# Third and last attention: scores from 12-bit halves in float32r, their rows spread by DMAs

## The chip, the cores and the metric

One core of one Trainium2 chip runs the kernel. The metric is the device time of one execution in microseconds. The core has TensorE (PE for its matmuls, PEld for its weight loads), VectorE (DVE), ScalarE (ACT), GpSimd (POOL) and SyncE (SP), each with a queue of its own that runs in order, and 16 DMA engines that all queues share. A DMA is issued by an instruction in one of these queues; here SP, ACT and POOL issue DMAs.

## The reference

The input x has 32 sequences of 128 tokens with 128 features. Four blocks follow each other, each an attention and a feed-forward layer with a gated residual. Only the third and the last attention matter here:

```python
# L2: one key head and one value head shared by 16 query heads of 8 features
qh = (q @ w_q).reshape(B, L, 16, 8).transpose(0, 2, 1, 3)
k, v = split(c @ w_kv)                       # 8 features each
attn = softmax(einsum('bhid,bjd->bhij', qh, k) / sqrt(8))

# L3: 16 heads of keys and values, a padding mask and a causal mask
scores = einsum('bhqd,bhkd->bhqk', q, k) / sqrt(8)
scores = where(mask + future != 0, -1e9, scores)
attn = softmax(scores)

x = x + tanh(g) * (attention(layernorm(x), context) @ wo)
```

In both layers the queries come from the normed x, keys and values from the context. Everything is fp32.

## The kernel before

**Stages.** Eight stages run one after the other and overlap at their ends: L0 (attention), F0, L1, F1 (feed-forward with quantised weights), L2 (attention), F2 (experts), L3 (attention), F3. All 32 sequences ("tiles" of 128 tokens) stay in SBUF. The three attentions L0, L2 and L3 share one program, `attention(layer)`, which each engine runs as `iteration(t)`; the tile of the softmax is t, the tile of the first scores t + 2, that of the output projection t - 2. Four tiles make a quad, and `quad(t, lead)` is the number of the quad that begins `lead` tiles ahead, in one iteration of four.

**Scores of one tile.** Each pair of head groups needs its scores twice: once as queries by keys, to find each row's maximum (banks 0 and 1, semaphore `t_s1`, read by DVE's `maxima`, L1744), and once as keys by queries, for the exponentials (banks 2 and 3, `t_s2`, read by ACT's `exponentials`, L960). `pair_of_scores(u, g, v, f)` on PE does one half tile of both: the second kind for tile u and the first kind for tile v = u + 2. The heads of a group of four are told apart by zeros: `k_one` and `q_one` hold four copies of the keys and queries of a quad in which all but one head is multiplied by 0, so that one matmul of 32 partitions by 512 columns gives the scores of four heads (L1284 and L1287). Four such matmuls, one for each group of 32 partitions, follow each other directly. fp32 matmuls appear in the profile as two records. Then L1298 adds minus the maximum, in bf16 parts. In L3, L1274 and L1279 first write the masks into the banks, 16 bf16 matmuls of 32 partitions by 128 columns.

**What waits for what.** Banks 0 to 3 have one buffer: a pair's second kind waits for the exponentials of the pair before it (`t_ex`), its first kind for the maxima of the pair before it (`t_mx`). Between the pairs PE does the weighted values (`weighted_values`, L1316), the output projection and transposes, and once a quad the projections of the next quads: transposes of the normed x (L1382), queries (L1433), keys (L1389), values (L1438).

**ACT's work.** Besides the exponentials, ACT copies what PE projects from bank 5 into `q_all`, `k_all` and `vals`, and makes the four copies of the keys (L970) and of the queries (L976; in L2 only copies 2 and 3, DVE makes 0 and 1 at L1752). `q_all` and `k_all` have two buffers, one for each of two quads.

**Heads.** The first iterations of L2 (t from -10 to -3) are interleaved with the end of F1, by the tables `TENSOR_BETWEEN` and `SCALAR_BETWEEN`, those of L3 with the last expert slots of F2, by `LAST_HEAD`. DVE takes no part in these heads. SP issues no DMA in L2 and none in L3; in F2 it loads experts and rows, and in F3 it stores the output.

## Time and profile before

| | |
|---|---|
| median of three executions | 1081.1 us (1077.25 to 1084.16) |
| span of the profiled execution | 1082.4 us |
| L2, from its first exponentials to its last | about 482 to 668 us |
| L3, the same | about 813 to 1000 us |
| share of PE, DVE, ACT, POOL in the span | 84%, 69%, 63%, 43% |

The span is the time from the first to the last instruction of one profiled execution. It is 1.3 us above the median and inside the range of the three, so sums made against it carry over. A row of a timeline gives the start, the duration, the engine, the line, the operation and what it writes and reads; in brackets stands how long its engine was idle before it and who ended that.

### The profile page before, as it was taken

The numbers are of one execution on the slowest core, as the hardware profiler recorded it, in microseconds if no ns is written. First come the engines' busy times: TensorE is split into PE (matmuls) and PEld (weight loads), VectorE is DVE, ScalarE is ACT, GpSimd is POOL, SyncE is SP. The second block draws the span as 40 slices with busy tenths as digits, with TensorE's granted clock in tenths as the row PEclk, the third lists the DMA queues.
The fourth block names the chain that finished last, engine by engine and source line by source line (L and its number), as shares of the span: only waits on it lengthen the run. The fifth ranks groups of instructions, "written<-read, shape, count | busy, mean of one in ns | idle before, by whom it ended". The sixth has DMA issues, their size and how long they took to land.

```text
span 1082.4 us, 29166 instructions
## 1 busy us (share of the span) xinstructions
PE 913.5 (84%) x9573; PEld 567.0 (52%) x9573; DVE 743.3 (69%) x2005; ACT 684.9 (63%) x1499; POOL 468.1 (43%) x999
## 2 busy tenths in 40 slices
PE   2898888995667856689999989878999899999898
PEld 2744444442345523334555544678864445454698
DVE  2667767765996979967888886337527776666344
ACT  3556666654875656667777764545676677775466
POOL 5422357671124523410144434668651258885200
PEclk9999989996667957799999999999999999999999
DMA  6977677636799997000000000866820001110011
GB/s 175 166 87 100 51 96 86 81 49 135 178 135 165 162 164 94 1 1 2 2 6 12 16 12 12 232 173 188 259 66 22 2 3 41 41 42 2 9 35 36
DMA packets 300444, 84.95 MB, mean 78 GB/s; under 512 B 211930, under 2 KB 287098, under 8 KB 300315
## 3 DMA queue, kind: packets, MB, share of 16 engines
q1 hardware_dynamic: 293962, 67.11, 38.3%
q0 software_dynamic: 5488, 15.88, 4.5%
q8 instruction: 78, 1.28, 0.5%
q14 instruction: 52, 0.42, 0.1%
q10 hardware_dynamic: 864, 0.27, 0.1%
HBM read 50.70 MB, written 35.51 MB: 80 GB/s over the span
## 4 chain that ended last, share of the span: by engine, by line
PE 61%; DVE 22%; issue 8%; POOL 3%; ACT 3%; DMA 2%; SPq 1%; DVEq 0%; ACTq 0%; POOLq 0%
PE bank L1284 16%; DVE nmax L1744 8%; PE bank L1316 7%; PE bank L1406 3%; PE bank L1298 3%; PE bank L1650 3%; PE bank L1642 3%; PE bank L1608 3%; PE bank L1596 3%; DVE small L1926 2%; PE bank L1287 2%; PE bank L1415 2%; PE bank L1274 2%; DVE stats L1679 1%; DVE q_one L1958 1%
## 5 line engine op out<-in xcount | busy, mean ns | idle before, releaser
L1744 DVE TENSOR_REDUCE nmax<-bank 128x8 f32<-128x1024 f32 x192 | 234.8, 1223 | 124.7 <-PE bank L1287 123.2
L960 ACT ACTIVATE probs_space<-bank 128x1024 f32<-128x1024 f32 x192 | 196.5, 1023 | 148.6 <-PE bank L1298 147.6
L1284 PE MATMUL bank<-q_one,k_all 32*128 32x512 f32 x768 | 218.1, 637 | 29.9 <-DVE nmax L1744 26.5
L1287 PE MATMUL bank<-k_one,q_all 32*128 32x512 f32 x768 | 217.4, 640 | 2.2 <-DVE nmax L1744 0.9
L1316 PEld LDWEIGHTS bank<-probs_space,vals 128*32 128x32 f32 x3072 | 73.0, 110 | 123.6 <-issue 122.8
L1316 PE MATMUL bank<-probs_space,vals 128*32 128x128 f32 x3072 | 125.6, 282 | 0.2 <-ACT probs_space L960 0.2
L1284 PEld LDWEIGHTS bank<-q_one,k_all 32*128 32x128 f32 x768 | 62.0, 185 | 59.2 <-issue 57.3
L647 POOL TENSOR_TENSOR var_b<-stats 128x8 f32<-128x8 f32 (+3 forms) x33 | 7.4, 223 | 175.2 <-DVE stats L1679 173.9
L722 POOL CAST nmax_parts<-nmax 128x16 bf16<-128x16 f32 x64 | 12.6, 196 | 160.9 <-DVE nmax L1744 145.5
L970 ACT ACTIVATE k_one<-k_all,one_head 128x512 f32<-128x512 f32 x96 | 68.9, 722 | 20.8 <-DVE k_all L1768 19.3
L1298 PE MATMUL bank<-nmax_one,ones_bf 12*128 12x512 bf16 x384 | 78.6, 381 | 0.0
L1778 DVE TENSOR_TENSOR nmax_one<-bank,max_row 128x512 bf16<-128x512 bf16 x96 | 65.5, 682 | 2.7 <-PE bank L1363 2.7
L1679 DVE BATCH_NORM_STATS2 stats<-x 128x6 f32<-128x128 f32 x230 | 61.3, 287 | 4.2 <-DMA x<-in_x_dram 1.2
L1287 PEld LDWEIGHTS bank<-k_one,q_all 32*128 32x128 f32 x768 | 59.0, 185 | 5.3 <-issue 4.2
L880 POOL DMA_INDIRECT token_rows<-early,slot_row_int x46 | 48.5, 1054 | 29.5 <-DVE early L2114 19.0
L706 POOL TENSOR_TENSOR late<-bf_up,late 128x512 f32<-128x512 f32 x36 | 56.7, 1593 | 0.1
L654 POOL TENSOR_TENSOR var_a<-var_b,minus_half 128x8 f32<-128x8 f32 (+3 forms) x33 | 54.4, 1650 | 2.6
L1608 PE MATMUL bank<-moe_w,probs_space 128*128 x368 | 51.1, 283 | 4.1 <-DVE early L2114 3.7
L976 ACT ACTIVATE q_one<-q_all,one_head 128x512 f32<-128x512 f32 x80 | 54.5, 727 | 0.0
L1608 PEld LDWEIGHTS bank<-moe_w,probs_space 128*128 128x128 f32 x368 | 46.2, 197 | 5.1 <-issue 5.0
L1180 ACT ACTIVATE q_one<-bank,up_bias 128x128 f32<-128x128 f32 x128 | 36.5, 369 | 19.2 <-PE bank L1642 19.2
L865 POOL DMA_INDIRECT expert_rows<-late,dest_int x32 | 32.1, 1004 | 31.6 <-DVE dest_int L1850 24.5
(290 smaller groups left out, 2229.4 us busy)
## 6 DMA issues: line engine op xcount, KB each, us to landing
expert_rows<-zeros SPq DMA_DIRECT2D x8, 2322.0 KB, 38.4
context<-expert_w SPq DMA_DIRECT2D x31, 322.0 KB
k_one<-expert_w SPq DMA_DIRECT2D x15, 322.0 KB
late<-_L_ffn_down_weights_dram POOLq DMA_DIRECT2D x9, 512.0 KB, 5.4
late<-in_L_ffn_up_weights_dram POOLq DMA_DIRECT2D x9, 512.0 KB, 4.0
q_one<-expert_rows SPq DMA_DIRECT2D x46, 64.5 KB
q_scratch<-late SPq DMA_DIRECT2D x8, 256.0 KB
v_scratch<-moe_w SPq DMA_DIRECT2D x8, 256.0 KB
```

The source lines that it names most:

```text
L706: pool.tensor_tensor(tmp(i), half(src, i % 2), weight, ALU.mult).then_inc(S("bf_step"), 1)
L960: act.activation(probs[:, 2 * g:2 * g + 2, :, :].rearrange("k g i q -> k (g i q)"), bank_pair[1][:, :, :].rearrange("k g f -> k (g f)"), A ...
L970: act.activation(k_one[:, c % 2, i, :], k_all[:, c % 2, :], ACT.Copy, scale=one_head[:, i:i + 1]).then_inc(S("t_k1"), 1)
L976: act.activation(q_one[:, c % 2, i, :], q_all[:, c % 2, :], ACT.Copy, scale=one_head[:, i:i + 1]).then_inc(S("t_q23" if i >= 2 else "t_q01 ...
L1284: pe.matmul(bank[2 + s], group(k_all, u, 2 * g + s), group(q_one, u, 2 * g + s), start=not masked, stop=False)
L1287: m = pe.matmul(bank[s], group(q_all, v, 2 * f + s), group(k_one, v, 2 * f + s), start=not masked, stop=True)
L1298: m = pe.matmul(bank[2 + s], ones_bf[first:last, :], nmax_one[first:last, u % 2, :, :], start=False, stop=True)
L1316: m = pe.matmul(bank[4][32 * j:32 * j + 32, g * P:(g + 1) * P], v[:, first:first + VW], probs[:, 2 * g + j // 2, j % 2 * 2 + s, :], start= ...
L1608: m = pe.matmul(bank[(4, 6)[(t - 1) % 2]][:, 0:P], slot_hid[:, (t - 1) % 2, c * P:(c + 1) * P], w2[:, bass.ds(expert[t - 1] * HID + c * P, ...
L1679: dve.bn_stats(stats[:, u, :], x[:, u * P:(u + 1) * P]).then_inc(S("stats"), 1)
L1744: dve.tensor_reduce(nmax[:, u % 2, 0, :].rearrange("q (g i) -> q g i", i=HG)[:, 2 * g:2 * g + 2, :], bank_pair[0][:, :, :].rearrange("q g ...
L1778: dve.tensor_tensor(nmax_one[:, (t + 1) % 2, :, :], over_blocks(bank[6][:, 3 * P:4 * P].bitcast(BF16)[:, 0:P], HG), max_row[:, :].unsqueez ...
```

## The change

In L2 and L3 (`own` in the code) a number is cut in two: `upper` is the fp32 value with its low 12 bits cleared, the other half is the rest. The product of a query and a key is the sum of four products of halves, and these four fill the partitions that were zeros before: in the operands `q_rows` and `k_rows` partition 32 * group + 4 * feature + n holds half `Q_HALVES[n]` of the query or `K_HALVES[n]` of the key. The matmuls read them as float32r. `SCORE_SCALE` moves into the exponentials' `scale`.

- `k_one` and `q_one` copies (L970, L976, L1752) are gone in L2 and L3. DVE splits each quad's keys and queries instead (`halves`: one `bitwise_and`, one `subtract`, each 128 x 512), and holds each once: `q_all` and `k_all` now have one buffer, with the two halves in it.
- DMAs of 32 partitions by 512 fp32 numbers (64 KB), from SBUF to SBUF, spread the halves. For each quad ACT issues 16 for the queries, 8 at the end of iteration `quad(t, 4)` and 8 at the end of `quad(t, 3)`, each time behind the exponentials of that iteration. SP issues those of the keys, 4 per quad in L2 and 16 in L3.
- PE waits for all of a quad's DMAs (`operands_in`) before the first scores of that quad, in `quad(t, 2)`. ACT waits for the same before it overwrites the staging for the next quad (`staging_free`), in the same iteration. The operands have three buffers.
- The matmuls: in L2 the second kind stays one matmul of 512 columns per group (keys are shared), the first kind becomes four of 128 columns. In L3 both kinds become four of 128 columns per group, so a pair has 16 matmuls in place of 4.
- The order of a quad's projections becomes keys (lead 7), transposes and queries (6), values (4). Heads start earlier, and DVE takes part in them. Attention weights are loaded with their heads reordered, in four DMAs each where it was one (nine more, on SP, near 265 us).

```diff
+        def rows_of_quad(layer, c):                         # SP
+            if c >= QUAD_BUFFERS:
+                sp.wait_ge(S("t_s2"), 2 * QT * (quads + c - QUAD_BUFFERS + 1))
+            for upper in (1, 0):
+                done += 1
+                sp.wait_ge(S("t_half"), done)
+                for n in range(4):
+                    for i in range(1 if layer == "L2" else HG):
+                        if K_HALVES[n] == upper:
+                            sp.dma_start(rows_of(k_rows, layer, c)[n:P:4, i, :].bitcast(F32),
+                                         k_all[HR * at:HR * at + HR, upper, :]).then_inc(S(name), 16)
 
+        def query_rows(c, upper):                           # ACT
+            act.wait_ge(S("t_half"), 4 * (own_quads + c + 1) - upper)
+            for n in range(4):
+                for i in range(HG):
+                    if Q_HALVES[n] == upper:
+                        act.dma_start(rows_of(q_rows, layer, c)[n:P:4, i, :].bitcast(F32),
+                                      q_all[HR * i:HR * i + HR, upper, :]).then_inc(S(name), 16)
 
         def iteration(t):                                   # ACT
-            past(act, "t_s2", 2 * (tiles + QT * (c - 1)))
+            staging_free(c)                                 # waits for operands_in of quad c - 1
             act.wait_ge(S("t_kp"), quads + c + 1)
-            act.activation(k_all[:, c % 2, :], quad_bank(c), ACT.Copy).then_inc(S("t_kn"), 1)
+            act.activation(k_all[:, 0, :], quad_bank(c), ACT.Copy).then_inc(S("t_kn"), 1)
...
             if live(t):
                 exponentials(t, 1)
+            if own and quad(t, 4) is not None:
+                query_rows(quad(t, 4), 1)
+            if own and quad(t, 3) is not None:
+                query_rows(quad(t, 3), 0)
 
+        def scores_of_heads(u, g, v, f):                    # PE
+            for s in range(2):
+                if live(u) and shared_keys:
+                    pe.matmul(bank[2 + s], operand(k_rows, u, 2 * g + s, 0),
+                              operand(q_rows, u, 2 * g + s, slice(0, HG)), start=not masked, stop=False)
+            for i in range(HG):
+                at = slice(i * P, i * P + P)
+                for s in range(2):
+                    if live(u) and not shared_keys:
+                        pe.matmul(bank[2 + s][:, at], operand(k_rows, u, 2 * g + s, i),
+                                  operand(q_rows, u, 2 * g + s, i), start=not masked and i == 0, stop=False)
+                    if live(v):
+                        m = pe.matmul(bank[s][:, at], operand(q_rows, v, 2 * f + s, i),
+                                      operand(k_rows, v, 2 * f + s, 0 if shared_keys else i),
+                                      start=not masked and i == 0, stop=i == HG - 1)
...
                 if live(v):
-                    pe.wait_ge(S("t_qa"), quads + v // QT + 1)
-                    pe.wait_ge(S("t_k1"), HG * (quads + v // QT + 1))
+                    name, landed = operands_in(layer, v // QT)
+                    pe.wait_ge(S(name), landed)
 
+        def halves(both, copied, c, done):                  # DVE
+            dve.wait_ge(S(copied), quads + c + 1)
+            dve.tensor_scalar(both[:, 1, :].bitcast(I32), both[:, 0, :].bitcast(I32), UPPER_BITS, None,
+                              ALU.bitwise_and).then_inc(S("t_half"), 1)
+            dve.wait_ge(S("t_half"), done + 1)
+            dve.tensor_tensor(both[:, 0, :], both[:, 0, :], both[:, 1, :], ALU.subtract
+                              ).then_inc(S("t_half"), 1)
...
-        if layer not in SPLIT_BY_POOL and quad(t, 2) is not None:
-            one_head_queries(quad(t, 2), 0)
+        if own and quad(t, 6) is not None:
+            halves(k_all, "t_kn", quad(t, 6), 0)
+        if own and quad(t, 5) is not None:
+            halves(q_all, "t_qa", quad(t, 5), 2)
```

## Rows read from the trace of the kernel before

**Rows 1.** The page's first section: busy time, share of the span, instructions of each engine.

```profile
PE 913.5 (84%) x9573; PEld 567.0 (52%) x9573; DVE 743.3 (69%) x2005; ACT 684.9 (63%) x1499; POOL 468.1 (43%) x999
```

**Rows 2.** Windows of F1, L2, L3: length, busy us per engine, clock, DMA share, GB/s.

```profile
320.00:480.00 160.00, 112.01 (x653) 69.75 (x654) 134.15 (x464) 102.00 (x258) 62.55 (x147) 0.76 0.81 104
560.00:600.00 40.00, 38.57 (x429) 20.78 (x430) 33.48 (x94) 29.24 (x57) 19.18 (x44) 1.00 0.05 15
860.00:900.00 40.00, 37.47 (x619) 19.42 (x618) 28.01 (x49) 30.62 (x54) 21.72 (x44) 1.00 0.05 16
```

**Rows 3.** Windows of line L1298 alone: PE busy, PEld busy, clock, DMA share, GB/s.

```profile
560.00:600.00 40.00, 5.21 (x26) 1.53 (x26) 1.00 0.05 15
860.00:900.00 40.00, 5.12 (x27) 1.43 (x26) 1.00 0.05 16
```

**Rows 4.** PE timeline in L3: start, duration, line, operation (first rows of their runs).

```profile
870.87 0.21 PE L1274 MATMUL bank<-quant_bf,future_rep 32*128 32x128 bf16 x1
...
871.09 0.64 PE L1284 MATMUL bank<-q_one,k_all 32*128 32x512 f32 x1
...
872.00 0.40 PE L1298 MATMUL bank<-nmax_one,ones_bf 12*128 12x512 bf16 x2
...
873.69 0.21 PE L1274 MATMUL bank<-quant_bf,future_rep 32*128 32x128 bf16 x1 [0.40 <-DVE nmax L1744]
```

**Rows 5.** PEld timeline in L3: one weight load of bf16, one of fp32.

```profile
871.01 0.09 PEld L1279 LDWEIGHTS bank<-ident_blocks_bf,past_rep 32*128 32x128 bf16 x1
871.04 0.18 PEld L1284 LDWEIGHTS bank<-q_one,k_all 32*128 32x128 f32 x1
```

**Rows 6.** ACT timeline in L3.

```profile
872.44 1.02 ACT L960 ACTIVATE probs_space<-bank 128x1024 f32<-128x1024 f32 x1 [1.17 <-PE bank L1298]
...
875.27 1.02 ACT L960 ACTIVATE probs_space<-bank 128x1024 f32<-128x1024 f32 x1 [0.38 <-PE bank L1298]
877.37 0.60 ACT L998 ACTIVATE vals<-bank 128x512 f32<-128x512 f32 x1 [1.08 <-PE bank L1438]
878.84 1.02 ACT L960 ACTIVATE probs_space<-bank 128x1024 f32<-128x1024 f32 x1 [0.87 <-PE bank L1298]
```

**Rows 7.** ACT timeline in L2, exponentials of two half tiles, copies left out.

```profile
585.97 1.02 ACT L960 ACTIVATE probs_space<-bank 128x1024 f32<-128x1024 f32 x1 [0.41 <-PE bank L1298]
...
589.58 1.02 ACT L960 ACTIVATE probs_space<-bank 128x1024 f32<-128x1024 f32 x1 [0.69 <-PE bank L1298]
```

**Rows 8.** PE timelines of L2: a pair in full run, and the first scores.

```profile
588.19 0.69 PE L1284 MATMUL bank<-q_one,k_all 32*128 32x512 f32 x1
...
471.61 1.13 PE L1287 MATMUL bank<-k_one,q_all 32*128 32x512 f32 x4 [0.52 <-issue]
```

**Rows 9.** DVE timeline in L2.

```profile
590.58 0.69 DVE L1778 TENSOR_TENSOR nmax_one<-bank,max_row 128x512 bf16<-128x512 bf16 x1
591.18 0.48 DVE L1752 TENSOR_SCALAR q_one<-q_all,one_head 128x512 f32<-128x512 f32 x1
```

**Rows 10.** Timelines of the queues ACT and SP: DMA issues, start and duration.

```profile
2.75 0.45 ACTq L924 DMA_DIRECT2D bo_row<-in_L_xattn_bo_dram  x1
3.23 0.45 ACTq L925 DMA_DIRECT2D bk_row<-in_L_xattn_bk_dram  x1
...
269.79 0.32 SPq L460 DMA_DIRECT2D mask_nat<-in_mask_BxS_ik_dram  x1
```

**Rows 11.** Lines L585 (SBUF to DRAM), L460 (DRAM to 32 partitions): ns min/median/max, us to landing.

```profile
L585 SPq DMA_DIRECT2D out_dram<-x x32: 338/343/373, 1022.1 to 1080.4; - x32
...
DMA to landing us min/median/max: 1.5/1.5/2.2
...
DMA to landing us min/median/max: 2.3/2.3/2.3
```

**Rows 12.** The page's fifth section: ACT's copies of keys and of queries.

```profile
L970 ACT ACTIVATE k_one<-k_all,one_head 128x512 f32<-128x512 f32 x96 | 68.9, 722 | 20.8 <-DVE k_all L1768 19.3
L976 ACT ACTIVATE q_one<-q_all,one_head 128x512 f32<-128x512 f32 x80 | 54.5, 727 | 0.0
```

202 lines of the change are left out of this document (137 added, 65 removed).

## The prediction

> **What bounds the kernel now.** I read the page's busy shares first, then windows by stage, then timelines of PE, ACT and DVE in the middle of L2 and L3. PE has the largest share, 913.5 of 1082.4 us [rows 1]. In the middle of L2 it is busy 38.6 of 40 us, DVE 33.5, ACT 29.2; in L3 37.5, 28.0 and 30.6, at full clock in both [rows 2]. L1298 has two groups per half tile, so four records per tile: 26 records in 40 us of L2 are 6.5 tiles, 6.15 us a tile; 27 in L3 make 5.93 us [rows 3]. PE sets the pace in both, and in L2 DVE is close behind (33.5 / 6.5 = 5.15 us a tile, against 28.0 / 6.75 = 4.15 in L3). PE's idle time comes from a ring: a pair's scores wait for the maxima and exponentials of the pair before. In L3 the exponentials begin at 872.44 and end at 873.46; the next pair begins at 873.69, only 0.23 us later [rows 4, 6]. Whatever is put between these two delays PE.
>
> **The matmuls, removed and added.** Four score matmuls of a pair take from 871.09 to 872.00, 0.91 us, so 1.82 us a tile [rows 4]. After the change no row shows a float32r matmul. Lower bound: the masks of the same pair are 16 bf16 matmuls of 32 partitions by 128 columns and take from 870.87 to 871.09, 0.22 us [rows 4], the very shape of L3's new scores. Upper bound: 0.91 us as now, if four-byte operands keep today's rate. Weight loads count too: there are 16 where four fp32 matmuls had 8 records of them, and one of fp32 lasts 0.18 us against 0.09 for bf16 [rows 5]. I take twice the masks' time, 0.45 us, for that ratio; it is nearer the lower end because the shape is the masks'. PE saves 2 x (0.91 - 0.45) = 0.92 us a tile.
>
> In L3 the next limits are away from that (DVE 4.15, ACT 30.6 / 6.75 = 4.5 us a tile [rows 2, 3]), but the ring with the maxima takes a part; I count 0.82 us a tile, 3.3 us a quad. In L2 DVE is the next limit. It gets two `bitwise_and` (nearest row 0.48 us) and two subtractions (0.69) a quad and loses two copies of 0.48 [rows 9]: 2.34 - 0.96 = +1.4 us a quad, 5.15 + 0.35 = 5.5 us a tile busy, and its ops wait for each other. Between 6.15 and 5.5 I count 0.4 us a tile, 1.6 us a quad.
>
> **ACT's copies, removed.** In L3 eight a quad, in L2 six, of 0.72 us [rows 12], 5.8 and 4.3 us of ACT. They lie in ACT's idle time (it idles 0.38 to 1.17 us before exponentials [rows 6]) and PE hardly waits for them, so their removal is worth nothing by itself. It frees the time that the DMAs need.
>
> **ACT's DMAs, added.** An issue occupies the queue that issues it: on ACT 0.45 us at a pitch of 0.48 (2.75 to 3.23), on SP 0.32 us for 32 partitions [rows 10] and 0.34 us for SBUF to DRAM [rows 11]. No row has SBUF to SBUF. I take 0.34 and a gap of 0.04, so 0.38; bounds 0.36 and 0.48. A burst of eight is 3.0 us (2.9 to 3.8), and 16 a quad are 6.1 us, about what the copies took. But the copies could be fitted in one by one; a burst stands in the ring. Landing after the last issue: 1.5 us for SBUF to DRAM, 2.3 for DRAM to 32 partitions [rows 11]; I take 2.0. Whether the queue may issue while the exponentials ahead of it still run, no row shows: if so, up to 0.9 us of a burst is hidden. I take half, 0.5.
>
> **The Trainium skill on issue cost.** "DMA: Bandwidth & Descriptors", Issuing engines are not separate DMA queues, says that the sequencer time to initiate a DMA is usually small relative to the DMA itself. By it the sum would be the matmuls' gain alone, without these bursts. The rows bear it out only in part: 0.32 to 0.48 us against 1.5 to 2.3 us for one, but a burst of eight is longer than a landing. It is rival A.
>
> *Second burst (lower halves), end of iteration `quad(t, 3)`.* The next thing on PE is the first pair that reads the new quad, and it waits for the landing. From the end of the exponentials: 3.0 - 0.5 + 2.0 = 4.5 us. In L3 PE would have begun 0.23 us after them [rows 4, 6], and somewhat later now that pairs are shorter: a stall of 4.2 us. In L2 the gap now is 588.19 - 586.99 = 1.2 us [rows 7, 8] and DVE still has a backlog then: 3.3 us. Behind PE's wait stand its weighted values, transposes and everything DVE and ACT get from them. ACT's own wait for the staging ends at the same landing and adds nothing.
>
> *First burst (upper halves), end of iteration `quad(t, 4)`.* It delays the next exponentials. The gap between two exponentials with the values' projection between them is 878.84 - 876.29 = 2.55 us in L3, less 0.60 for the copy of the values [rows 6], less 0.46 for the shorter pair: 1.5 us free against 3.0 - 0.5. 1.0 us of delay. In L2 it is 589.58 - 586.99 = 2.6 us [rows 7], by the same way 0.9 us.
>
> **SP's DMAs.** 4 or 16 a quad, 1.5 or 6 us of a queue that is empty in L2 and L3, ordered two iterations before PE's wait. Hidden; without that cover they would add to the 4.5 us. 32 DMAs of 64 KB a quad are 2.1 MB in about 25 us, where DMA carries 15 GB/s now [rows 2]. The extra weight loads are 9 x 0.48 = 4 us of SP before the expert table, needed 400 us later: hidden too.
>
> **Heads.** The first quad's DMAs lie ahead of each stage. In L2 the first scores come at 471.61 [rows 8], soon after keys and queries are copied; instead of 6 copies of 0.72 there are 16 issues (6.1 us) and a landing of 2.0: 6.1 + 2.0 - 4.3 = about +4 us. In L3 two bursts fall between expert slots in place of eight copies, 6.1 against 5.8 us, but in two lumps: +2 us. Bounds 0 and 12 for both.
>
> **The sum.** Seven quads of each stage have their bursts inside it.
>
> - L3: -3.3 + 4.2 + 1.0 = +1.9 a quad, x 7 = +13 us.
> - L2: -1.6 + 3.3 + 0.9 = +2.6 a quad, x 7 = +18 us.
> - Heads +6 us. Total +37 us: span 1082.4 + 37 = 1119, and 1.3 less for the median: **1118 us**.
>
> With issue 0.36, landing 1.5, the burst hidden by 0.9 and scores at 0.22 the same sum per quad is, in L3, -3.3 - 1.8 + (2.9 - 0.9 + 1.5 - 0.3) + 0.5 = -1.4, and in L2 about 0: -10 us, heads 0: 1071. With issue 0.48, landing 2.3 and nothing hidden, a burst is 0.8 us longer and 0.5 us more of it shows: the second adds 1.6, the first 1.3 us. L3 +1.9 + 2.9 = +4.8, L2 +2.6 + 2.9 = +5.5, together +72 us, heads +6: 1159.
>
> **Rivals.**
>
> *A, the DMAs cost nothing* (issue is cheap on a busy ACT queue, or the rows land before PE asks). For it: ACT idles about a quarter of L3, and SP's DMAs are ordered early. Against it: PE asks 0.23 us after the exponentials behind which eight issues stand. Then only the gain stays: 8 x 3.3 + 8 x 1.6 = 39 us, 1042 us. It ends faster, and decides once a burst and its landing take less than about 1.5 us together. 15%.
>
> *B, a 128-column float32r matmul is no faster than fp32.* 0.91 us a pair remains. For it: operands still have four bytes and weights load 16 times. Against it: 16 x 128 columns in four strips took 0.22 us in bf16. The gain of 39 us is gone: 1118 + 34 (seven quads each) = 1152 us. 15%.
>
> *C, the stall costs the clock.* PE would idle 4 us in every quad, and in F1, where it is busy 112 of 160 us, the granted clock was 0.76 [rows 2], so part of the time at the 1.2 GHz level. If in each of 14 quads some 3 us of PE work ran at half speed, that is 1.5 x 14 = +21 us: 1139 us. Against it: PE's share would still be about 0.8. 10%.
>
> *D, within 1%.* The mild ends of issue, landing and cover meet: bursts half hidden, about 1071 to 1092 us. 15%.
>
> **How the numbers follow.** The likeliest case, with C's milder part, has 45%: 1093 to 1145 by the bounds of single terms, and 1118 in the middle. A to D have 15, 15, 10, 15. A range of 1071 to 1160 leaves out A and what of B comes with long bursts. Faster by over 1% (about what a measurement of this kernel can tell from no change): A and a tail of D, 0.17. Within 1%: 0.15. Slower: 0.68.
>
> **What would show it.** In the profile after: eight DMA issues in ACT's queue behind every fourth exponentials, twice, at a pitch near 0.38 us; PE idle about 4 us before the first score matmul of each quad, ended by a DMA; L1298's records at a pace of about 6.8 us a tile in L2 and 6.4 in L3 on average, with iterations between bursts shorter than 6.15 and 5.93; a pair's scores in about 0.45 us. I am wrong if ACT's issues are much shorter, if no DMA ends a wait of PE, or if a pair still takes 0.9 us.

## The result and the profile after

The changed kernel takes **1245.5 us** (median of 4 runs, 1237.9 to 1250.3), the kernel before beside it 1081.6. The ratio is 1.150, 95% interval [1.1445, 1.1555]. The prediction was 1118 us in a range of 1071 to 1160: the sign is right and the loss is more than four times as large. The profiled execution has a span of 1236.1 us, against 1082.4, at a mean granted clock of 0.805 against 0.929.

The page of the kernel after: busy time, the clock slice by slice, the exponentials and the new DMA groups.

```profile
PE 970.9 (79%) x10213; PEld 670.9 (54%) x10213; DVE 770.0 (62%) x2053; ACT 622.7 (50%) x1387; POOL 469.2 (38%) x999
...
PEclk9999999967696766677576658999888777776899
...
L1044 ACT ACTIVATE probs_space<-bank 128x1024 f32<-128x1024 f32 x192 | 196.5, 1023 | 188.4 <-PE bank L1429 188.2
...
q_rows<-q_all ACTq DMA_DIRECT2D x256, 64.0 KB
k_rows<-k_all SPq DMA_DIRECT2D x160, 64.0 KB
```

Windows of 40 us in the middle of L2 and L3, in the columns of [rows 2]. There TensorE, VectorE and ScalarE were busier and the clock was 1.00; here TensorE is busy 33.1 and 29.1 us of 40, and at a clock of 0.67 and 0.75 that busy time holds less work.

```profile
600.00:640.00 40.00, 33.10 (x344) 23.57 (x345) 25.75 (x69) 18.28 (x35) 12.38 (x28) 0.67 0.20 54
1010.00:1050.00 40.00, 29.08 (x488) 19.62 (x486) 20.43 (x34) 16.31 (x29) 25.61 (x44) 0.75 0.36 102
```

The same windows, the group that answers to L1298 of [rows 3] (four a tile, and the mean of one): 20 and 18 records are 5 and 4.5 tiles, so about 8.0 and 8.9 us a tile where there were 6.15 and 5.93.

```profile
L1429 PE MATMUL bank<-nmax_one,ones_bf 12*128 12x512 bf16 x20 | 4.9, 477 | 0.0
...
L1429 PE MATMUL bank<-nmax_one,ones_bf 12*128 12x512 bf16 x18 | 4.4, 473 | 0.0
```

**Where the 153.7 us are.** From the first and last exponentials of each stage (ACT timeline, L960 before and L1044 after):

| us | before | after | difference |
|---|---|---|---|
| start of L2 | 483.6 | 496.7 | +13.1 |
| L2, first to last | 188.5 | 249.4 | +60.9 |
| L2 to L3 | 142.2 | 157.1 | +14.9 |
| L3, first to last | 193.1 | 257.8 | +64.7 |
| after L3 | 75.0 | 75.0 | 0 |

A quad has eight gaps between starts of exponentials. The table has their means over the third to sixth quad. The first burst falls in gap 2 and the second in gap 4.

| gap, us | 1 | 2 | 3 | 4 | 5 | 6 | 7 | 8 | quad |
|---|---|---|---|---|---|---|---|---|---|
| L2 before | 2.75 | 2.62 | 2.95 | 3.61 | 2.91 | 3.39 | 3.25 | 2.70 | 24.2 |
| L2 after | 3.15 | **6.10** | 2.66 | **7.37** | 3.69 | 3.60 | 2.78 | 3.18 | 32.5 |
| L3 before | 3.00 | 2.83 | 2.82 | 3.57 | 3.34 | 3.04 | 3.27 | 2.80 | 24.7 |
| L3 after | 2.58 | **6.46** | 2.95 | **8.60** | 4.09 | 4.03 | 2.35 | 3.07 | 34.1 |

**One pair of bursts, read through.** ACT timeline of the kernel after in L3 (start, duration; ACTq is the issuing of DMAs):

```profile
1041.81 1.02 ACT L1044 ACTIVATE probs_space<-bank 128x1024 f32<-128x1024 f32 x1 [0.50 <-PE bank L1429]
1041.87 5.58 ACTq L1069 DMA_DIRECT2D q_rows<-q_all  x8
1047.56 0.60 ACT L1095 ACTIVATE vals<-bank 128x512 f32<-128x512 f32 x1 [4.72 <-issue]
1048.05 1.02 ACT L1044 ACTIVATE probs_space<-bank 128x1024 f32<-128x1024 f32 x1
...
1051.08 1.02 ACT L1044 ACTIVATE probs_space<-bank 128x1024 f32<-128x1024 f32 x1 [1.19 <-PE bank L1429]
1051.14 4.99 ACTq L1069 DMA_DIRECT2D q_rows<-q_all  x8
1057.63 0.60 ACT L1087 ACTIVATE k_all<-bank 128x512 f32<-128x512 f32 x1 [5.53 <-DMA q_rows<-q_all]
1059.65 1.02 ACT L1044 ACTIVATE probs_space<-bank 128x1024 f32<-128x1024 f32 x1 [1.43 <-PE bank L1429]
```

The PE timeline of the same time, the first masks of two pairs, the first scores of the pair before them, and what lies around them:

```profile
1042.82 1.06 PE L1574 MATMUL bank<-l_wkv,contextT 128*128 128x128 f32 x8
...
1044.02 0.30 PE L1372 MATMUL bank<-q_rows,k_rows 32*128 32x128 f32 x1
...
1044.50 0.39 PE L1429 MATMUL bank<-nmax_one,ones_bf 12*128 12x512 bf16 x2
1044.82 0.64 PE L1447 MATMUL bank<-probs_space,vals 128*32 128x128 f32 x16
...
1049.12 0.28 PE L1403 MATMUL bank<-ffn_wT,future_rep 32*128 32x128 bf16 x1 [3.34 <-ACT probs_space L1044]
...
1050.97 1.08 PE L1447 MATMUL bank<-probs_space,vals 128*32 128x128 f32 x16
...
1057.70 0.26 PE L1403 MATMUL bank<-ffn_wT,future_rep 32*128 32x128 bf16 x1 [3.21 <-issue]
...
1058.94 0.68 PE L1429 MATMUL bank<-nmax_one,ones_bf 12*128 12x512 bf16 x2
```

Issuing starts 0.06 us after the exponentials start, so it runs beside them. The eight issues last 5.6 us in the first burst and 5.0 in the second, 0.70 and 0.62 us each. The values' copy and the next exponentials stand behind the first burst, and PE stands behind the exponentials (3.34 us). The gap with the second burst is 8.57 us: 0.06 + 4.99 of issue, 1.50 until the last rows have landed (1056.13 to 1057.63), 0.07, then 1.24 for masks and scores and 0.71 to the exponentials. The sixteen matmuls of L1447 last 0.64 us ahead of the pause and 1.08 us behind it: PE came back at the half level, 1.2 GHz: the granted clock was 0.50 from 1047.12 to 1053.95, and PE had stood still for 1.3 us when it fell.

### The profile page after: what moved, and what is told of

Same layout as the page of the kernel before. It is cut to its first block and busy times, and to the rows that moved or that the text cites. A ratio compares the mean times of both kernels' runs of the same rounds, so it can differ in the third digit from the quotient of the medians.

```text
span 1236.1 us, 30518 instructions
## 1 busy us (share of the span) xinstructions
PE 970.9 (79%) x10213; PEld 670.9 (54%) x10213; DVE 770.0 (62%) x2053; ACT 622.7 (50%) x1387; POOL 469.2 (38%) x999
## 5 line engine op out<-in xcount | busy, mean ns | idle before, releaser
L1044 ACT ACTIVATE probs_space<-bank 128x1024 f32<-128x1024 f32 x192 | 196.5, 1023 | 188.4 <-PE bank L1429 188.2
L1447 PE MATMUL bank<-probs_space,vals 128*32 128x128 f32 x3072 | 151.5, 326 | 1.4 <-issue 1.4
L1447 PEld LDWEIGHTS bank<-probs_space,vals 128*32 128x32 f32 x3072 | 86.0, 125 | 77.1 <-issue 71.8
L1375 PE MATMUL bank<-k_rows,q_rows 32*128 32x128 f32 x1024 | 112.5, 352 | 4.6 <-DMA q_rows<-q_all 4.6
L1375 PEld LDWEIGHTS bank<-k_rows,q_rows 32*128 32x128 f32 x1024 | 94.3, 255 | 8.0 <-DMA q_rows<-q_all 5.6
L1429 PE MATMUL bank<-nmax_one,ones_bf 12*128 12x512 bf16 x384 | 93.8, 466 | 0.0
L1415 PE MATMUL bank<-q_one,k_all 32*128 32x512 f32 x256 | 73.4, 640 | 20.0 <-DVE nmax L1880 16.9
L1917 DVE TENSOR_TENSOR nmax_one<-bank,max_row 128x512 bf16<-128x512 bf16 x96 | 65.7, 684 | 21.3 <-PE bank L1498 19.5
L1366 PE MATMUL bank<-q_rows,k_rows 32*128 32x512 f32 x128 | 43.9, 677 | 42.0 <-issue 22.6
L1418 PE MATMUL bank<-k_one,q_all 32*128 32x512 f32 x256 | 73.4, 646 | 1.7 <-DVE nmax L1880 0.9
L958 POOL DMA_INDIRECT token_rows<-early,slot_row_int x46 | 48.8, 1060 | 42.5 <-DVE early L2258 33.1
L1944 DVE RECIPROCAL o_inv<-bank 128x16 f32<-128x16 f32 x96 | 24.5, 256 | 54.9 <-PE bank L1546 54.6
L1744 PE MATMUL bank<-moe_w,probs_space 128*128 x368 | 51.2, 285 | 4.2 <-DVE early L2258 3.6
L1366 PEld LDWEIGHTS bank<-q_rows,k_rows 32*128 32x128 f32 x128 | 16.7, 247 | 68.8 <-issue 52.6
L1372 PE MATMUL bank<-q_rows,k_rows 32*128 32x128 f32 x512 | 52.6, 331 | 0.0
L1744 PEld LDWEIGHTS bank<-moe_w,probs_space 128*128 128x128 f32 x368 | 46.9, 200 | 4.9 <-issue 4.9
```

The costliest lines, as they stand in the source:

```text
L1044: act.activation(probs[:, 2 * g:2 * g + 2, :, :].rearrange("k g i q -> k (g i q)"), bank_pair[1][:, :, :].rearrange("k g f -> k (g f)"), A ...
L1366: pe.matmul(bank[2 + s], operand(k_rows, u, 2 * g + s, 0), operand(q_rows, u, 2 * g + s, slice(0, HG)), start=not masked, stop=False)
L1372: pe.matmul(bank[2 + s][:, at], operand(k_rows, u, 2 * g + s, i), operand(q_rows, u, 2 * g + s, i), start=not masked and i == 0, stop=False)
L1375: m = pe.matmul(bank[s][:, at], operand(q_rows, v, 2 * f + s, i), operand(k_rows, v, 2 * f + s, 0 if shared_keys else i), start=not masked ...
L1415: pe.matmul(bank[2 + s], group(k_all, u, 2 * g + s), group(q_one, u, 2 * g + s), start=True, stop=False)
L1418: m = pe.matmul(bank[s], group(q_all, v, 2 * f + s), group(k_one, v, 2 * f + s), start=True, stop=True)
```

## The experiments

Ratios are to the kernel before, measured beside each on the same chip (its median was 1074 to 1083 us), with 95% intervals, so they are what is to be compared. In the code, `...` stands for lines left out.

### All DMAs of the halves on SyncE

```diff
-                    if own and quad(t, 4) is not None:
-                        query_rows(quad(t, 4), 1)
-                    if own and quad(t, 3) is not None:
-                        query_rows(quad(t, 3), 0)
...
+                for upper in (1, 0):
+                    sp.wait_ge(S("t_half"), 4 * (own_quads + c + 1) - upper)
+                    for n in range(4):
+                        for i in range(HG):
+                            if Q_HALVES[n] == upper:
+                                sp.dma_start(rows_of(q_rows, layer, c)[n:P:4, i, :].bitcast(F32),
+                                             q_all[HR * i:HR * i + HR, upper, :]).then_inc(S(name), 16)
```

> The changed kernel with one edit: the queries' 16 DMAs per quad are issued by SyncE behind the keys', none by ScalarE. In the changed kernel an issue lasts 0.62 us (median), eight take 5.15 us between two exponentials, and L2 and L3 go at 8.1 and 8.5 us a tile. Theory S (the bursts in ScalarE's queue stand in the ring of scores and exponentials, and that is the loss): L2 returns to 5.7 us a tile, bound by VectorE; in L3 SyncE must issue 32 x 0.62 = 20 us a quad, about 5.2 us a tile. Time about 1236 - 32 x 2.4 - 32 x 3.2 = 1060 us. Theory K (TensorE's granted clock, 0.6 to 0.8 in L2 and L3 of the changed kernel, is the loss and comes from the shorter passes themselves): the clock stays below 0.8, L2 and L3 stay above 7 us a tile, time above 1160 us. Theory M (both: the bursts make TensorE idle, and the idle lowers the clock): clock back to about 1.0 and the time of theory S.

1164.2 us, ratio 1.076 [1.070, 1.083]: half of the loss is gone, about 80 us. Gaps 2 and 4 are 4.63 and 4.26 us in L2, 4.02 and 6.30 in L3. In L3 SyncE's queue is now the late one. Its timeline there shows it issuing without a stop from 934.48 to 953.94, 19.5 us of a quad of 28:

```profile
934.48 8.33 SPq L597 DMA_DIRECT2D k_rows<-k_all  x11
942.85 11.09 SPq L604 DMA_DIRECT2D q_rows<-q_all  x16
```

### Without the queries' DMAs, then without any, from the fourth quad on

```diff
-                        query_rows(quad(t, 4), 1)
+                        query_rows(quad(t, 4), 1) if quad(t, 4) < QUAD_BUFFERS else None
...
-                        query_rows(quad(t, 3), 0)
+                        query_rows(quad(t, 3), 0) if quad(t, 3) < QUAD_BUFFERS else None
```

> The changed kernel with the queries' DMAs left out from the fourth quad of each stage on (ScalarE issues them for quads 0 to 2 only, later quads read the queries of an earlier quad; that part of the computation is wrong then). The keys' DMAs stay on SyncE. Within each stage quads 0 to 2 have the bursts and quads 3 to 7 do not. Theory S: quads 3 to 7 go at 5.7 us a tile in L2 and 5.0 in L3, at full clock; time about 1236 - 5 x 4 x (2.4 + 3.5) = 1118 us. Theory K: the clock stays low in quads 3 to 7 as well, above 7 us a tile, time above 1180 us.

1168.4 us, ratio 1.078 [1.072, 1.084]. The scores here use the rows of an earlier quad. Quads that still have bursts last 7.2 to 8.9 us a tile, the others up to 7.2.

Then, in `rows_of_quad`, the keys' too:

```diff
+                if c >= QUAD_BUFFERS:
+                    return
```

> The changed kernel with the DMAs of the halves, those of the queries and those of the keys, left out from the fourth quad of each stage on (the scores then use the rows of earlier quads, so part of the computation is left out). VectorE's halves, ScalarE's copies and the new matmuls stay. Theory T (all of the loss is in the DMAs, their issue and landing): from the fourth quad on VectorE (22 us busy a quad in L2) and TensorE (some 20 us of work at full clock in L3) set the pace, quads of 22 to 23 us, the stages' other three quads as in the changed kernel; total about 1245 - 5 x 10 - 5 x 12 = 1135 us. Rival U (float32r in 128 columns brings the clock down whatever the DMAs do): quads of 6.5 to 7.1 us a tile as without the queries' DMAs, total about 1165 us at a clock of 0.83. Rival K (the keys' DMAs on SyncE hold L3 back, nothing holds L2): L2 as without queries' DMAs (26 to 28 us a quad), L3 down to 22 to 23 us a quad: 1145 us.

1151.9 us, ratio 1.077 [1.069, 1.085]. Beside 1.078 without the queries' DMAs, the keys' DMAs on SyncE cost nothing that shows; U's and K's times (1165, 1145) are as near as T's (1135), and the quads decide: L2 26.6, L3 27.5 us in the middle, not 22 to 23. T said that all of the loss lies in the DMAs, and it is out: with none at all the new scores are slower than the old ones. How much so, the quads also say. From first to last exponentials L2 is 26.8 us longer than before and L3 23.9; 33 of these 51 us lie in the first two quads of each stage, which still have their bursts, and 18 in the others. The windows of the middle show the clock at 0.78 and 0.76, and the DVE timeline in L3 shows the halves themselves, long while GpSimd works.

```profile
977.10 1.57 DVE L1890 TENSOR_SCALAR q_all<-q_all 128x512 int32<-128x512 int32 x1
978.70 1.86 DVE L1893 TENSOR_TENSOR q_all<-q_all 128x512 f32<-128x512 f32 x1
```

GpSimd's timeline of the same time:

```profile
975.33 4.68 POOL L786 TENSOR_TENSOR late<-bf_up,late 128x512 f32<-128x512 f32 x3
```

The same two take 0.42 and 0.69 us in L2, and here 17 of 32 in L3 do too. In the changed kernel itself 29 of the 32 in L3 take that long: GpSimd's operations seldom fell beside them. The maxima of the next half tile stand behind the two.

### What an issue costs

48 DMAs of six forms put on SyncE's queue in L2 of the kernel before, eight of each.

```diff
+                sp.wait_ge(S("t_s1"), 2 * NT + 8)
...
+                            0: (context[n % 4:P:4, at], contextT[0:32, at]),
+                            1: (context[0:32, at], contextT[0:32, at]),
...
+                        sp.dma_start(to, frm).then_inc(S("form"), 16)
```

> The kernel before with 48 more DMAs on SyncE, which is idle in L2, eight of each form, each form landed before the next: SBUF to SBUF of 32 rows of 2 KB to every fourth partition (the change's form); the same to 32 neighbouring partitions; 128 rows of 512 B; 32 rows of 512 B to every fourth partition; SBUF to DRAM, 32 rows of 2 KB; SBUF to SBUF of 128 rows of 2 KB. Nothing reads what they write. If the issue's length comes from the step in partitions, the first and fourth forms last 0.62 us and the second 0.35. If it comes from both sides lying in SBUF, all but the fifth last 0.6. If it comes from bytes, the fourth is short and the sixth long. Time unchanged within 1%, since SyncE has nothing else to do there.

1080.2 us in one execution, no different from before, so SyncE's queue had room. The rows of its line, from the view of one line (ns min/median/max, first and last start):

```profile
L551 SPq DMA_DIRECT2D context<-contextT x40: 498/595/2018, 490.5 to 529.2; - x40
L551 SPq DMA_DIRECT2D token_rows<-contextT x8: 340/426/561, 519.0 to 522.3; - x8
```

SBUF to SBUF is about 0.6 us whether the partitions have a step or not and whether 16, 64 or 256 KB move (eight of 256 KB took 5.76 us in all); SBUF to DRAM 0.43. The row that I had taken for it, [rows 11], is of the second kind.

### The faster scores without anything else

Keys and queries as before, written and read as float32r, 512 columns, no halves and no DMAs. The lower bits of the scores are left out.

```diff
-                            pe.matmul(bank[2 + s], group(k_all, u, 2 * g + s), group(q_one, u, 2 * g + s),
+                            pe.matmul(bank[2 + s], group(k_all_r if own else k_all, u, 2 * g + s), group(q_one_r if own else q_one, u, 2 * g + s),
```

> The kernel before with the scores of L2 and L3 read as float32r and nothing else changed: the copies with one head stay, matmuls of 512 columns, no halves and no DMAs (the scores lose their lower bits). It measures what a one-pass score matmul is worth by itself. Theory S: a pair takes about 0.3 us where it took 0.91, L3 goes from 5.93 to about 5.0 us a tile and L2 to 5.5, full clock, time about 1082 - 32 x 0.9 - 32 x 0.6 = 1034 us. Theory K: with the passes gone the clock falls in L2 and L3, and the time is 1080 us or more.

1053.8 us, ratio 0.973 [0.969, 0.978]. The gain is about 2.0 us a quad (22.4 and 22.6 for 24.2 and 24.7), nearly all of it in the six gaps without a burst in the changed kernel (16.2 and 16.4 us for 18.0 and 18.3). From its first score to the first matmul that adds minus the maximum, a pair takes 0.33 us in the lines below (full clock; L3's median is 0.32) against 0.91 [rows 4].

In the changed kernel L2's pairs, with two matmuls of 512 columns and eight of 128, take 0.31 to 0.34 us by the same measure. L3's, with sixteen of 128 columns, take 0.48 (1044.02 to 1044.50 above, and the median of 29 pairs at full clock). At the half level they take 0.57 to 0.60 and 0.90: there L3's new pair is as long as the fp32 one was at full clock.

```profile
885.59 0.48 PE L1298 MATMUL bank<-q_one_r,k_all_r 32*128 32x512 f32 x1
...
885.92 0.41 PE L1312 MATMUL bank<-nmax_one,ones_bf 12*128 12x512 bf16 x2
```

### The same DMAs in four lumps

Sixteen issues a quad stay on ScalarE's queue, four at each of four places, the last of them one half tile earlier than the old second burst.

```diff
+                    if own and quad(t, 4) is not None:
+                        query_rows(quad(t, 4), 1, 2)
+                    if own and quad(t, 3) is not None:
+                        query_rows(quad(t, 3), 0, 2)
                     if live(t):
                         exponentials(t, 1)
+                    if own and quad(t, 5) is not None:
+                        query_rows(quad(t, 5), 1, 0)
                     if own and quad(t, 4) is not None:
-                        query_rows(quad(t, 4), 1)
-                    if own and quad(t, 3) is not None:
-                        query_rows(quad(t, 3), 0)
+                        query_rows(quad(t, 4), 0, 0)
```

> The changed kernel with the same 16 DMAs a quad on ScalarE's queue, but in four lumps of four in place of two of eight: after the exponentials of the iteration with quad(t, 5), ahead of and after the second exponentials of quad(t, 4), ahead of the second exponentials of quad(t, 3). None stands right ahead of TensorE's wait for the new quad. In the changed kernel the two gaps between exponentials in which a burst lies are 6.10 and 7.37 us in L2, 6.46 and 8.60 us in L3, against 2.62, 3.61, 2.83 and 3.57 before. Theory L (what costs is the lump in the ring and the landing right ahead of the new quad): these two gaps fall to 3.5 to 4.5 us, four lumps of 2.6 us find 1 us of idle time each and add 1.5 us each: quads of 28 to 30 us in place of 32.5 and 34.1, 1245 - 14 x 4 = about 1190 us. Theory Q (ScalarE's queue is simply full, 14 us of copies and exponentials and 10.3 us of issue a quad, and each issue is added to the path wherever it stands): 1245 within 10 us. Rival: the lumps ahead of the exponentials delay them in full, and quads grow: over 1255 us.

1169.0 us, ratio 1.079 [1.075, 1.083]. Theory L, and more of it than expected: 76 us come back though ScalarE issues as many DMAs as before. Gaps 2 and 4 are 3.76 and 3.37 us in L2, 3.98 and 2.97 in L3. The lumps are not free where they stand now: gaps 1 and 3 are 4.03 and 4.49 us in L2, 4.03 and 3.44 in L3, for 2.75, 2.95, 3.00 and 2.82 before. Theory Q, a full queue, is out.

### A third of the issues, by way of DRAM

The staged halves (the queries', in L3 the keys' too) go out in one DMA and return in four of 256 KB each, all on SyncE: 9 and 10 a quad in place of 20 and 32. The same rows arrive.

```diff
+                sp.dma_start(home.rearrange("p (b f) -> p b f", b=2), staging[:, :, :]).then_inc(S("bounced"), 16)
+                sp.wait_ge(S("bounced"), 16 * len(bounces))
+                for n in range(4):
+                    at = slice(QT * P * halves[n], QT * P * (halves[n] + 1))
+                    sp.dma_start(rows_of(rows, layer, c)[n:P:4, :, :].bitcast(F32),
+                                 home[:, at].rearrange("(i p) f -> p i f", i=HG)).then_inc(S(name), 16)
```

> The changed kernel with fewer DMAs: the staged halves of the queries (and in L3 of the keys) go to DRAM in one DMA and come back in four, each with 32 partitions of four heads (256 KB), all on SyncE's queue; 9 DMAs a quad in L2 and 10 in L3 in place of 20 and 32, ScalarE has none. The same bytes arrive at the same rows. Theory N (it is the number of issues, 0.62 us each, that costs; in the kernel with all of them on SyncE, 1164 us, the gap ahead of the new quad in L3 was 6.3 us because SyncE issued for 20 of 28 us): that gap falls to about 3.5 us, L3 to 26 us a quad, L2 as there: 1164 - 8 x 2.5 = about 1145 us, and the head of L2 is 3 us shorter. Rival M (the path through DRAM has two landings in line, 1.6 us out and 2.5 us or more back, 256 KB each; they arrive late): gap ahead of the new quad 6 us or more in both stages, 1165 to 1200 us. Rival P (the pace is set by TensorE's clock and VectorE anyway): 1155 to 1165 us.

1127.9 us, ratio 1.044 [1.041, 1.048]. Without fills it is the best form of the change, though it moves more bytes. Gap 4 in L3 is 3.9 us: theory N. Of its span of 1120.6 us, 38 more than before, 9.6 are ahead of L2, 12.5 between the stages, 9.6 in L2 and 6.5 in L3.

### Does the clock cost, or only show?

Matmuls that compute nothing, put where TensorE stands still.

```diff
+                    if own and live(u) and live(v) and f == 1 and v >= QT:
+                        past(pe, "t_mx", 2 * (tiles + v) + (1 - f))
+                        fill_wait(FILL[layer].get(v % QT, 0), 0)
```

> The changed kernel, with extra matmuls that compute nothing (bf16, 512 columns, 0.216 us each at full clock) put on TensorE where it stands still: 14 (L2) and 16 (L3) of them ahead of the first pair of a new quad, 8 and 12 ahead of the pair after the first burst. No DMA and no wait is changed. Theory T (the bursts make pauses, and after the pauses TensorE's work runs at the half level, which then costs about as much again): in the profile of the changed kernel a quad of L3 has 26.5 us of busy TensorE at a granted clock of 0.75, the same work at full clock would be some 20 us. If the clock comes back to about 0.95 the kernel falls by up to 5 to 6 us a quad, 14 quads: 1245 - 75 = about 1170 us, and the bursts alone keep quads at 28 us. Rival V (the clock is only a symptom: the ring waits for ScalarE and DMA, slower matmuls lie under these waits): clock up, time within 10 us of 1245. Rival U (the clock falls for a reason that pauses do not set, the float32r matmuls themselves): clock stays near 0.75 and the time grows by the fills, 1245 + up to 15 us.

1222.2 us, ratio 1.137 [1.132, 1.142]. In the edit, 8 (L2) and 14 (L3) fills stand ahead of the pair after the first burst, 12 and 16 ahead of the first pair of a new quad. A good part of the clock comes back, the time hardly does. Windows of the middle of L2 and L3:

```profile
600.00:640.00 40.00, 34.48 (x371) 22.78 (x369) 24.54 (x67) 17.77 (x35) 12.32 (x28) 0.82 0.19 52
1010.00:1050.00 40.00, 35.14 (x556) 22.63 (x559) 24.32 (x41) 16.97 (x31) 20.83 (x39) 0.87 0.28 82
```

The six gaps without a burst fall from 19.1 to 17.7 us in both stages, but gap 2 grows, by 0.8 us to 6.90 and by 1.6 to 8.07. The fills did that. They stand ahead of the pair after the first burst, which in the changed kernel ran while the burst was being issued (1043.81 to 1044.50); now that pair begins when they end, and ScalarE, whose burst and copy are over at 1067.45, waits 1.64 us for it. Two rows of its PE timeline in L3 and two of its ACT timeline:

```profile
1064.48 3.56 PE L1295 MATMUL bank<-ones_bf 128*128 128x512 bf16 x14
1067.97 0.23 PE L1407 MATMUL bank<-ffn_wT,future_rep 32*128 32x128 bf16 x1
...
1066.85 0.60 ACT L1096 ACTIVATE vals<-bank 128x512 f32<-128x512 f32 x1 [5.19 <-issue]
1069.09 1.02 ACT L1045 ACTIVATE probs_space<-bank 128x1024 f32<-128x1024 f32 x1 [1.64 <-PE bank L1433]
```

Of the 75 us that theory T allowed, 14 came, net of some 17 us (seven quads of 0.8 and of 1.6) that the fills cost in gap 2. So with bursts in place the clock was worth at most about 30 us: for more than half of T's sum it is V, the slow matmuls lie under waits.

One fill a pair in L2 and two in L3, in the kernel with all DMAs on SyncE:

```diff
+                    if own and live(u) and live(v) and v >= QT:
+                        past(pe, "t_mx", 2 * (tiles + v) + (1 - f))
+                        fill_wait(FILL[layer], 0)
```

> All DMAs of the halves on SyncE's queue, as in the earlier kernel of that kind (1164 us, clock 0.835), plus one (L2) or two (L3) empty matmuls of 0.216 us ahead of every pair of scores, after the wait for the maxima. Theory T' (what is left of the loss there is TensorE's clock, which fell because TensorE was busy only 0.82 to 0.92 of the time): clock back to about 0.95 or more, quads of 22 to 23 us in L2 and 24 to 26 us in L3 instead of 26 to 31 and 26 to 32: about 1164 - 20 - 15 = 1130 us. Rival V (fills cost more than the clock gives, since the maxima set the pace): 0.22 us x 8 and 0.43 x 8 a quad are 1.7 and 3.5 us, up to + 14 + 28 = 1205 us. Rival U (float32r itself lowers the clock): clock stays near 0.83, time 1165 to 1205.

With all DMAs on SyncE the same medicine does more: 1125.7 us, ratio 1.052 [1.047, 1.057] against 1.076 without, 27 us, near the time of T' (34). Its quads are not: in the middle they go from 27.6 to 24.9 us in L2, where T' had 22 to 23, and from 28.3 to 29.2 in L3, where it had 24 to 26 and gap 4, SyncE's, is still 6.1 us. From first to last exponentials L2 is 9 us shorter and L3 10. In the middle of its L2 and L3:

```profile
600.00:640.00 40.00, 35.11 (x459) 23.27 (x457) 36.00 (x105) 22.02 (x42) 17.93 (x47) 0.92 0.22 60
930.00:970.00 40.00, 32.96 (x579) 20.40 (x577) 25.63 (x45) 18.02 (x32) 27.04 (x50) 0.96 0.34 97
```

The same lines with `fill_wait(1, 0)`, in the kernel by way of DRAM and in the one with float32r scores alone:

> The kernel with the halves by way of DRAM on SyncE's queue, and one empty matmul of 0.216 us ahead of each pair of scores in L2 and L3, as brought the kernel with all DMAs on SyncE from 1.076 to 1.052 of the kernel before. Theory T' (the clock is what is left once the bursts are gone): about 0.03 below the ratio without the fills, clock 0.9 or more in the middle quads. If the DRAM way is late (rival M), the fills lie in the wait and the gain is under 0.01. A ratio under 1.00 would need quads of 23 us in both stages and a head of L2 as before, which no theory here gives: the head alone was 12 us longer in every kernel with the halves.

1126.1 us, ratio 1.038 [1.033, 1.043], against 1.044 [1.041, 1.048] without: the intervals overlap, and T' had said 0.03.

> The kernel before with its score matmuls in float32r (512 columns, one pass, no halves and no DMAs; lower bits of the scores are left out), which took 1054 us, plus one empty matmul of 0.216 us ahead of every pair of scores of L2 and L3. There, three quads of 16 show a granted clock under 0.9 and others 0.92, at a PE share of about 0.88. Theory T (pauses cost the clock, and a fill gives it back): all quads at 1.00, quads of 21 us in L2 and 22 us in L3 instead of 21 to 25 and 22 to 25: 1054 - 15 = 1039 us. Rival V (a fill lies in the path between the maxima and the scores): + 0.2 us x 8 a quad, 14 quads, 1054 + 24 = 1078 us. Within 5 us of 1054: both, or neither.

1043.4 us, ratio 0.971 [0.966, 0.976], against 0.973 without: the same. The fourth to sixth quads of L2 are at 1.00 and last 22.2 us each, where without fills they lasted 24.9, 20.9 and 23.0, so their sum falls by 2 us; in L3 no such gain shows.

### Without DMAs and without the halves

From the fourth quad on VectorE's two operations work on 8 of 512 columns, in the kernel without DMAs; then the same with one or two fills a pair. The scores' lower halves are stale there.

```diff
+                    n = QT * P if c < QUAD_BUFFERS else 8
-                    dve.tensor_tensor(both[:, 0, :], both[:, 0, :], both[:, 1, :], ALU.subtract
+                    dve.tensor_tensor(both[:, 0, 0:n], both[:, 0, 0:n], both[:, 1, 0:n], ALU.subtract
```

> The changed kernel without any DMA of the halves from the fourth quad of each stage on (1152 us, ratio 1.077), and now VectorE's two operations on each staged operand work on 8 of 512 columns from there too, so nearly all of the making of the halves is left out there. What stays is the new score matmuls with ScalarE's copies. In the kernel without the DMAs, the two gaps between exponentials with the halves in them are 4.43 and 4.63 us in L3 against 3.04 and 2.80 before; the bitwise_and took 0.75 and 1.04 us and the subtraction 1.31 and 1.67 us there on average where GpSimd was running its 1.57 us operations, against 0.42 and 0.69 without. Theory H (the halves stand between the maxima, in the ring, and that is most of what is left): L3 quads fall from 27.3 us by 3 to 3.5 to 24, L2 from 26.6 by 1.5 to 2.2, over five quads each 25 us: about 1127 us. Rival T' (TensorE's clock is what is left; with less to wait for, TensorE idles less): the clock rises to 0.9 and more, 1115 us or less. Rival (other engines' order sets the pace, neither): over 1142 us.

1148.5 us (1141.9 to 1172.1), ratio 1.057 [1.052, 1.061], against 1.077 [1.069, 1.085] with the halves. That is some 20 us by these ratios and 14 by the medians of the same executions (1.059 and 1.072 of the kernel before), which lean less on one long execution; H had 25. Where they come from can't be read: the profiled execution is its longest, with L3 quads of 27.3 us and L2's of 25.9, at a clock of 0.83 and 0.64.

> The same kernel, without DMAs and without nearly all work on halves from the fourth quad on, plus one or two empty matmuls of 0.216 us ahead of each pair of scores. Theory T': clock at 0.95 or more in the middle quads, quads of 22 to 23 us in both stages, as the kernel before with float32r scores and the same fills (22.2 and 22.5 us): about 1105 us. If the clock cost nothing here: 0 to 15 us more than without fills.

1135.8 us, ratio 1.051 [1.044, 1.058], which overlaps 1.057 [1.052, 1.061] without fills; T' had said about 1105 us. At a clock of 1.00 in both windows the quads are 23.6 and 24.9 us; T' had said 22 to 23.

```profile
590.00:630.00 40.00, 35.90 (x497) 23.04 (x495) 34.17 (x104) 24.58 (x49) 18.47 (x50) 1.00 0.04 12
940.00:980.00 40.00, 36.94 (x757) 23.78 (x749) 31.06 (x51) 22.30 (x40) 34.65 (x61) 1.00 0.13 42
```

## Why the prediction was right in sign and wrong in size

By its own terms, seven quads of each stage:

| us | predicted | measured |
|---|---|---|
| both bursts: 7 x (3.3 + 0.9) and 7 x (4.2 + 1.0); gaps 2 and 4 | +66 | 7 x 7.2 + 7 x 8.7 = +111 |
| gain of the scores: 7 x 1.6 and 7 x 3.3; the other six gaps | -34 | 7 x 1.1 + 7 x 0.8 = +13 |
| heads | +6 | 13.1 + 14.9 = +28 |
| sum | +37 | +153 |

The gain of the scores lies in all eight gaps, so what a burst costs is somewhat more than its row says and what the other gaps lost somewhat less. Two steps failed, of about the same size: the price of an issue (45 us in the first row) and the gain of the scores with the clock left out of the sum (47 us in the second). The heads are 22 us more.

**The bursts: mechanism right, issue mis-sized.** The places, the order of waits and the landing (2.0 taken, 1.5 measured) were as described, and the burst does run beside the exponentials, by nearly all of their 1.0 us, better than the 0.5 taken. The price of an issue was wrong: 0.62 to 0.70 us, where I took 0.38 and an upper bound of 0.48. "No row has SBUF to SBUF" stood there, and I then bounded it with rows of other kinds as if these bounded it. A burst of eight is 5.0 to 6.1 us in the stages (median 5.1), above the 3.8 of my worst case. With 5.1, the whole cover of 1.0 and the landing of 1.5 my own terms give 2.6 + 4.4 us a quad in L2 and 2.6 + 5.3 in L3, 104 us in place of 66, near the 111 measured; with 4.2 us more in each head the sum is about 1164 us, just outside the range; most of the other 80 us lies elsewhere. The four lumps and the way through DRAM show that position and number of the issues set the loss, not ScalarE's busy time.

**The scores: priced about right, worth less.** A pair takes 0.31 to 0.34 us in L2 and 0.48 in L3 against my 0.45, so PE saves about 5 and 3.4 us a quad at full clock. As whole float32r operands, at 0.32 us a pair and nearly full clock, the scores bring 1.8 us a quad in L2 and 2.1 in L3. In L2 that is about my 1.6. In L3 I had 3.3 of 3.7 saved, and here 2.1 came of 4.7: "the next limits are away from that" was the wrong reading, since the step from scores to maxima to the next scores is latency, not busy time. My own row says so: the pair at 873.69, which I set against the end of the exponentials, had waited for the maxima (`[0.40 <-DVE nmax L1744]`, [rows 4]). In the DVE timeline of before, the maxima of L1744 last 1.23 us, and in L3 most of them stand behind a wait of 0.93 to 1.01 us for their scores: that round stays, however idle VectorE is.

In the changed kernel nothing of this gain is left: the six other gaps are 1.1 and 0.8 us a quad longer, not 1.6 and 3.3 shorter. The clock is part of it, for which the sum had no term. At the half level L3's pair takes 0.90 us, the time of the old one, and the fills brought these gaps back by 1.4 us a quad in each stage, 20 of the 47 us. The smaller gain in L3 is some 8 more. The rest is not assigned.

**The halves.** In L3 I costed VectorE's four operations at nothing because it was busy only 28 of 40 us. In the kernel without DMAs, taking nearly all of them away was worth 14 to 20 us over both stages; that they stand between two maxima is read from the timeline. How much of it is VectorE's time and how much clock is not separated. In the changed kernel the halves of L3 were mostly short (0.42 and 0.69 us), so there it may be less.

**The heads.** L2's, predicted +4: ACTq issues from 470.39 to 480.66, and the first scores are at 482.19 where they were at 471.61 [rows 8]; the other 2.5 us come after them, at a clock of 0.50. The issuing is 16 times 0.64 us, and the rows land 1.5 us behind it. But the issues are not all: with them on SyncE L2 begins at 496.3 us, and with nine DMAs in place of twenty, by way of DRAM, still at 493.2. L3's, predicted +2: two lumps, 869.08 to 874.15 and 874.89 to 881.39, stand in ScalarE's queue ahead of the gate activations of the expert slots and keep it for 11.6 us.

```profile
869.08 5.07 ACTq L1069 DMA_DIRECT2D q_rows<-q_all  x8
874.25 0.28 ACT L1248 ACTIVATE xn<-bank 128x128 f32<-128x128 f32 x1 [6.25 <-issue]
...
876.05 5.34 ACTq L1069 DMA_DIRECT2D q_rows<-q_all  x6
881.49 0.28 ACT L1248 ACTIVATE xn<-bank 128x128 f32<-128x128 f32 x1 [5.06 <-PE bank L1724]
```

"In place of eight copies" counted the time and not the queue it blocks. Yet this can't be what the 14.9 us are: with all DMAs on SyncE, from L2's last exponentials to L3's first it is 159.2 us, and by way of DRAM 154.8, with no lump on ScalarE, against 157.1 here and 142.2 before. What makes L3's head longer in all of them stays open.

**The rivals.** A, DMAs that cost nothing, fell. By the Trainium skill ("DMA: Bandwidth & Descriptors", Issuing engines are not separate DMA queues) the time to initiate a DMA is usually small beside the DMA; here eight issues of 0.62 us or more stood against one landing of 1.5 us, and the measurement decides. For the keys' DMAs on SyncE A held: without them nothing changed. B, a float32r matmul no faster than fp32, fell. C, the clock, was real: 0.50 to 0.74 in L2's quads and 0.61 to 0.82 in L3's, where it was 0.89 to 1.00. As it is worded, its sum was half of what it should be: 3 us of work at half speed cost 3 us more, not 1.5, so 42 us and not 21. What fills gave back was 14 us with the bursts (net of some 17 that they cost) and 27 with all DMAs on SyncE; in the three other kernels it was 3 to 7 us, with overlapping intervals. The clock comes on top of the bursts, not as an alternative.

**What stays open.** With neither DMAs nor halves and at full clock, quads are still 23.6 and 24.9 us against 22.4 and 22.6 of the kernel with whole float32r operands. In L3 eight pairs of 0.48 us in place of 0.32 are 1.3 us of the 2.3. Its fills are 2.6 us of PE a quad, which may be in the path. The order of projections and copies also differs; neither was tried apart.

**A version that beats both** is the kernel before with float32r scores: 0.973, and 0.971 with fills. It gives up the lower bits, for which the halves were made.

## What to carry to other kernels

Price a DMA issue from a row with the same two memories, and multiply by the burst: if no such row exists, measure it by itself before counting, because it holds up the queue that issues it. Put DMAs where nothing is queued behind them, in small lumps ahead of the last moment, or make fewer of them even if they move more. An engine's busy share tells which is next only where work does not go round in a ring; in a ring, count the steps. A fill that is to lift the clock must end before the wait that it lies in; where it ends later it is itself the delay.

## What the runs showed of the hardware

- An SBUF to SBUF issue took 0.60 us (median of 40, three sizes from 16 to 256 KB) on SyncE and 0.62 on ScalarE (median of 256); SBUF to DRAM 0.34 [rows 11] to 0.43 us. It runs beside an activation that was started before it.
- float32r scores of a pair, to the next matmul: at full clock 0.32 us as four matmuls of 512 columns, 0.31 to 0.34 as two of 512 and eight of 128, and 0.48 as sixteen of 128, against 0.91 in fp32. At the half level the last two are 0.57 to 0.60 and 0.90.
- VectorE's `bitwise_and` on 128x512 went from 0.42 to as much as 1.57 us and the subtraction from 0.69 to 1.86 and 2.19 while GpSimd ran its 1.57 us operations (L3 of the kernel without DMAs). The Trainium skill ("GPSIMD Engine Reference", Key points) says that the two share SBUF interfaces and that VectorE instructions with two SBUF inputs or in a 2-port mode contend. The trace agrees for the subtraction, which has two SBUF inputs; in which mode the `bitwise_and` ran, no run shows.
- A kernel whose TensorE work gets shorter can be given a lower clock: 0.96 and 0.91 in windows of the float32r kernel where the slower fp32 scores had 1.00 [rows 2], with TensorE busy 35.1 and 35.2 us of 40 where it was 38.6 and 37.5; a fill of 0.2 us a pair brought 1.00 in both, and no time.
